# Middle stage of a two-layer Mamba and expert kernel: batch 0's front end by halves, 48 gathers in one row, normalised rows turned back by TensorE

## What is computed

```python
mod = (_silu(L1_c) @ L1_wmod).reshape(L1_c.shape[0], 6, 1, -1)
sa, ca, ga, sb, cb, gb = (mod[:, 0], mod[:, 1], mod[:, 2], mod[:, 3], mod[:, 4], mod[:, 5])
h = _layernorm(x, axis=-1) * (1 + ca) + sa
x = x + ga * _L1_attn_ref(h, ...)
h = _layernorm(x, axis=-1) * (1 + cb) + sb
x = x + gb * _L1_ffn_ref(h, ...)
# _L1_attn_ref: one projection makes z, x|B|C and dt; causal convolution of 4 taps and SiLU on x|B|C;
#   softplus(dt + bias); chunked state recurrence; y * silu(z), RMS norm, output projection;
#   residual is the modulated h itself, then a layer norm with gain and bias
```

## Time and profile before

| | |
|---|---|
| median of 3 runs | 1202.22 us (1201.95 to 1204.38) |
| profiled execution, its own time | 1202.39 us |
| its span, first to last instruction | 1200.5 us |
| busy of the span: PE, DVE, ACT, POOL | 73%, 76%, 52%, 64% |
| mean granted TensorE clock | 0.849 of 2.4 GHz |
| DMA, mean | 100 GB/s |

### The profile page before, as it was taken

One profiled execution on the slowest core, in us unless ns is written; L12 is line 12 of the kernel. 1 busy time (PEld: TensorE's weight loads), 2 busy tenths in 40 slices (PEclk: granted clock), 3 DMA queues, 4 the chain that ended last, 5 costly groups with the idle time before them and its releaser, 6 DMA issues. The chain is left out here.

```text
span 1200.5 us, 14790 instructions
## 1 busy us (share of the span) xinstructions
PE 874.4 (73%) x4148; PEld 554.2 (46%) x4148; DVE 911.2 (76%) x1783; ACT 622.3 (52%) x1381; POOL 771.1 (64%) x518
## 2 busy tenths in 40 slices
PE   7898659886988687751999618787867977339930
PEld 4343324333433332231999603364554666239930
DVE  4896999799979999968677648495986978365512
ACT  4857535665566455525444302748385584246620
POOL 0896698879987999810777378475435445337546
PEclk8998889898999798985899958789987967559975
DMA  6643345434544464442233311211100120142223
GB/s 185 185 146 117 113 156 158 132 126 139 179 133 135 134 183 154 131 146 65 76 93 93 65 51 44 63 35 56 30 25 30 37 66 23 35 176 81 63 62 96
DMA packets 94072, 120.50 MB, mean 100 GB/s; under 512 B 12604, under 2 KB 51972, under 8 KB 93864
## 3 DMA queue, kind: packets, MB, share of 16 engines
q1 hardware_dynamic: 87336, 105.92, 28.6%
q0 software_dynamic: 6656, 13.64, 4.6%
HBM read 105.27 MB, written 14.25 MB: 100 GB/s over the span
## 5 line engine op out<-in xcount | busy, mean ns | idle before, releaser
L678 POOL TENSOR_TENSOR ma_bu<-ma_u,ma_row_b 128x1024 f32<-128x1024 f32 x128 | 299.6, 2363 | 24.8 <-DVE decay_ps L782 16.7
L411 PE MATMUL y_ps<-ma_h,ident 128*128 128x512 f32 x512 | 261.6, 642 | 53.8 <-POOL ma_h L688 34.7
L555 ACT ACTIVATE decay_ps<-ma_delta,negA 128x512 f32<-128x512 f32 x256 | 173.1, 687 | 101.5 <-DVE ma_h L792 98.4
L1208 POOL DMA_INDIRECT s_rows<-xs,take x112 | 124.6, 1112 | 108.2 <-POOLq L952 71.4
L411 PEld LDWEIGHTS y_ps<-ma_h,ident 128*128 128x128 f32 x512 | 98.1, 203 | 195.6 <-issue 98.2
L782 DVE TENSOR_TENSOR_SCAN decay_ps<-decay_ps,ma_bu 128x512 f32<-128x512 f32 x96 | 114.6, 1208 | 24.0 <-ACT decay_ps L555 21.4
L792 DVE TENSOR_TENSOR ma_h<-decay_ps,ma_row_c 128x512 f32<-128x512 f32 x192 | 127.5, 664 | 0.0
L1225 PE MATMUL s_up_ps<-s_xt,s_w 128*128 128x128 f32 x896 | 123.1, 282 | 0.0
L782 DVE TENSOR_TENSOR_SCAN decay_ps<-decay_ps,ma_carry,ma_bu 128x512 f32<-128x512 f32 x96 | 120.5, 1270 | 0.3 <-POOL ma_bu L678 0.3
L1225 PEld LDWEIGHTS s_up_ps<-s_xt,s_w 128*128 128x128 f32 x896 | 113.8, 199 | 0.0
L688 POOL TENSOR_TENSOR ma_h<-ma_h,ma_row_c 128x1024 f32<-128x1024 f32 x32 | 75.2, 2350 | 34.1 <-DVE ma_h L782 32.8
(11 more groups left out here) (317 smaller groups left out, 1798.5 us busy)
## 6 DMA issues: line engine op xcount, KB each, us to landing
ma_row_b<-bc_rows SPq DMA_DIRECT2D x128, 256.0 KB, 3.6
ma_row_c<-bc_rows SPq DMA_DIRECT2D x128, 256.0 KB, 3.3
mi_cs<-cs_rows SPq DMA_DIRECT2D x32, 256.0 KB, 3.3
ys<-s_outs SPq DMA_DIRECT2D x28, 256.0 KB
w<-in_experts SPq DMA_DIRECT2D x1, 4112.0 KB, 13.7
w<-in_experts SPq DMA_DIRECT2D x1, 3072.0 KB, 10.3
xs<-rows SPq DMA_DIRECT2D x4, 512.0 KB, 3.3
out<-X SPq DMA_DIRECT2D x8, 256.0 KB, 2.3
```

Of the source, the lines that this page charges most:

```text
L411: mm = pe.matmul(y_ps[:, j, :], m.ident[:], h[g % HS][:, j, :], start=False, stop=True, skip_group_check=True)
L555: act.activation(decay[s % DS][:], delta[b % 2][:, j, col(c)], ACT.Exp, scale=m.negA0[:, j, n:n + 1]).then_inc(decay_done, 1)
L678: pool.tensor_tensor(bu[g % BUS][:], u[b % 2][:, :, col(c)], both(row_b[g % BS]), ALU.mult).then_inc(bu_done, 1)
L1208: pool.indirect_dma_start(rows[s % ROWS][:], None, m.xs[layer], bass.IndirectOffsetOnAxis(ap=m.take[:, s:s + 1], axis=0)).then_inc(fetched ...
```

## The change

Batch 0's front end is taken out of the rounds and written out ahead of them, by halves of 512 tokens (4 tiles): combine, moments, root, normalise, transposes, raw and x pieces, taps and SiLU of the first half do not wait for the second. The rounds now start at 0. Combine, moments and normalise of batch 1 also stand ahead of the rounds; its transposes and raw pieces stand in steps 0 and 1 of round 0, its x pieces in steps 1 to 4, all its z pieces in step 5, its taps one step later. POOL issues the 48 gathers of batches 0, 1 and 2 first of all.

The rows with scale and shift are no longer made by POOL. PE transposes the modulated `hT` back, by halves (`back10`, `back11`), through the same two banks, and ACT copies them to `rows`. So `modulate`, four broadcast loads and two thirds of `scale_row` and `shift_row` go.

```diff
-LATE = (144, 176)
+LATE = (80, 112)
...
-                for dst, block in ((m.gate[:, 0, 1], 5), (m.gate[:, 1, 1], 11), (m.lng_gate[:], 12), (m.lnb_gate[:], 13),
-                                   (m.shift_row[:, 1], 6), (m.scale_row[:, 1], 7), (m.shift_row[:, 2], 9),
-                                   (m.scale_row[:, 2], 10)):
+                for dst, block in ((m.gate[:, 0, 1], 5), (m.gate[:, 1, 1], 11), (m.lng_gate[:], 12), (m.lnb_gate[:], 13)):
...
-    ROUNDS = range(-3, NBATCH + 2)
+    ROUNDS = range(NBATCH + 2)
+    FIRST_GATHERS = (0, 0, 2, 2, 3, 3, 3, 3)
...
+        if s == 1 and valid(b - 2):
+            out += [("back11", b - 2, 0), ("back11", b - 2, 1)]
         if s == 5 and valid(b + 2):
             out += [("n10", b + 2, 0), ("n10", b + 2, 1)]
+        if s == 6 and valid(b + 2):
+            out += [("back10", b + 2, 0), ("back10", b + 2, 1)]
         if s >= 6 and valid(b + 2):
             out += [("raw", b + 2, 2, s - 6), ("raw", b + 2, 3, s - 6)]
-        if valid(n):
+        if n == 1:
+            if s == 0:
+                out += [("n10", 1, 0), ("n10", 1, 1), ("raw", 1, 2, 0), ("raw", 1, 3, 0)]
+            if s == 1:
+                out += [("raw", 1, 2, 1), ("raw", 1, 3, 1)]
+            if s == 6:
+                out += [("back10", 1, 0), ("back10", 1, 1)]
+            if 1 <= s < 5:
+                out += [("x", 1, (s - 1) // 2, (s - 1) % 2)]
+            if s == 5:
+                out += [("z", 1, j, c) for j in range(HALVES) for c in range(NCOL)]
+        elif valid(n):
...
+    halves = [[("raw", 0, 2, c), ("raw", 0, 3, c), ("x", 0, 0, c), ("x", 0, 1, c)] for c in range(NCOL)]
+    gates = [("z", 0, j, c) for j in range(HALVES) for c in range(NCOL)]
...
             def store_normed(n):
-                sp.wait_ge(modulated11, 2 * n + 2)
+                sp.wait_ge(piece_read, read("back11", n, 1))
...
+            for n in range(3):
+                for i in range(2 * GROUP * GROUPS):
+                    gather(n, i)
...
+                elif kind in ("back10", "back11"):
+                    r = key[2]
+                    pe.wait_ge(piece_read, read("n10" if kind == "back10" else "n11", n, r))
+                    for t in range(r * GROUP, (r + 1) * GROUP):
+                        mm = pe.transpose(bank[:, t % GROUP * P:(t % GROUP + 1) * P], m.hT[:, n, PAD + t * P:PAD + (t + 1) * P],
+                                          m.ident[:])
...
+            piece(("n10", 0, 0))
+            for key in halves[0]:
+                piece(key)
+            piece(("n10", 0, 1))
+            time_steps(0)
+            for key in halves[1][:3]:
+                piece(key)
+            pe.wait_ge(dtv_done, 1)
+            sums(0)
+            for key in halves[1][3:] + gates:
+                piece(key)
+            pe.wait_ge(cum_done, 1)
+            overlap(0)
+            turn(0)
+            for key in rows_back:
+                piece(key)
...
+                elif kind in ("back10", "back11"):
+                    first = n * BT + key[2] * GROUP
+                    ins = act.activation(m.rows[:, first:first + GROUP, :], bank[:].rearrange("p (t d) -> p t d", t=GROUP),
+                                         ACT.Copy)
...
+            root_half(0)
+            read_piece(("n10", 0, 0))
+            for key in halves[0]:
+                read_piece(key)
+            root_half(1)
+            read_piece(("n10", 0, 1))
+            for key in halves[1][:2]:
+                read_piece(key)
+            soften(0)
+            read_piece(halves[1][2])
+            exps(0)
+            for c in range(NCOL):
+                if c == 1:
+                    read_piece(halves[1][3])
+                    for key in gates:
+                        read_piece(key)
+                act.wait_ge(piece_read, read("x", 0, 1, c))
+                act.wait_ge(conv_step, (c + 1) * 2 * TAPS)
+                for j in (2, 3, 0, 1):
+                    xs = xbc[0][j][:, col(c)]
+                    silu = act.activation(xs, xs, ACT.Silu, bias=m.cb1[:, j:j + 1])
+                    if c == 1:
+                        silu.then_inc(silu_done, 1)
+            gate(0)
+            spans(0)
+            decay(0)
+            for key in rows_back:
+                read_piece(key)
+            root(rstd["n10"][:], rstd["n10"][:], n10_var, normed(1), logs, n10_rstd)
...
+            for c in range(NCOL):
+                part = range(c * GROUP, (c + 1) * GROUP)
+                combine(0, c)
+                dve.wait_ge(combined, c + 1)
+                moments(m.X, "n10", n10_var, part)
+                normalize(0, "n10", n10_rstd, c + 1, n10_xn, part)
+            for k in range(TAPS - 1):
+                convolve_half(0, k)
+            bias_steps(0)
+            convolve_half(0, TAPS - 1)
+            make_steps(0)
+            convolve_half(1, 0)
+            cumulated(0)
+            for k in range(1, TAPS):
+                convolve_half(1, k)
+            last_steps(0)
+            combine(1, 0)
+            masked(0)
+            combine(1, 1)
+            inputs(0)
+            dve.wait_ge(combined, 2 * GROUPS)
+            moments(m.X[:, tiles(1), :], "n10", n10_var)
+            normalize(1, "n10", n10_rstd, normed(1), n10_xn)
...
+                    tap = s - 1 if b == 0 else s
+                    if 0 <= tap < TAPS and valid(b + 1):
+                        convolve(b + 1, tap)
+                    if s in ((0, 2) if b == 0 else range(GROUPS)) and valid(b + 2):
+                        combine(b + 2, int(s > 0))
```

More of the change, by code:

```diff
@@ L1397, in pieces @@
         return out
+    halves = [[("raw", 0, 2, c), ("raw", 0, 3, c), ("x", 0, 0, c), ("x", 0, 1, c)] for c in range(NCOL)]
+    gates = [("z", 0, j, c) for j in range(HALVES) for c in range(NCOL)]
     place = {}
+    rows_back = [("back10", 0, r) for r in range(2)]
+    for key in [("n10", 0, 0)] + halves[0] + [("n10", 0, 1)] + halves[1] + gates + rows_back:
+        place[key] = len(place)
     for b in ROUNDS:
@@ L1515, in gather @@
                     ap=m.where[:, k, T:T + 1], axis=0)).then_inc(fetched[G % FETCH], 16)
[L1517 to L1525, removed]
-                                   ).then_inc(done, 1)
             def add_bias(n):
@@ L1554, in _ @@
                     if valid(b + 3):
-                        for i in range(sent, sent + GATHERS[s]):
+                        share = FIRST_GATHERS[s] if b == 0 else GATHERS[s]
+                        for i in range(sent, sent + share):
                             gather(b + 3, i)
-                        sent += GATHERS[s]
-                    if s == 7 and valid(b + 2):
-                        modulate(b + 2, 0, 0, read("n10", b + 2, 1), modulated10)
-                    if s == 0 and valid(b + 1):
-                        modulate(b + 1, 0, 1, read("n10", b + 1, 1), modulated10)
+                        sent += share
                     if s == 3 and valid(b):
                         add_bias(b)
-                    if s in (1, 2) and valid(b - 2):
-                        modulate(b - 2, 1, s - 1, read("n11", b - 2, 1), modulated11)
         @block.tensor
@@ L1799, in _, with root_half @@
                 act.activation(ex, below, ACT.Exp).then_inc(ex_done, 1)
+            def root_half(c):
+                half = rstd["n10"][:, c * GROUP:(c + 1) * GROUP]
+                root(half, half, n10_var, c + 1, logs, n10_rstd)
+            root_half(0)
[27 more added lines that the diff above has]
+            root(rstd["n10"][:], rstd["n10"][:], n10_var, normed(1), logs, n10_rstd)
             for b in ROUNDS:
@@ L1890, in convolve, with convolve_half @@
                     else:
-                        dve.wait_ge(conv_step, n * 2 * TAPS + 2 * (k - 1) + q + 1)
+                        dve.wait_ge(conv_step, convolved(n) + 2 * (k - 1) + q + 1)
                         dve.scalar_tensor_tensor(dst[:], src, tap, dst[:], ALU.mult, ALU.add).then_inc(conv_step, 1)
+            def convolve_half(c, k):
+                for q, j in enumerate(CONV):
+                    src, dst = raw[q][:, c * COL + k:c * COL + k + COL], xbc[0][j][:, col(c)]
+                    tap = m.tap1[:, j, k:k + 1]
+                    if k == 0:
+                        dve.wait_ge(piece_read, read("raw", 0, j, c))
+                        dve.tensor_scalar(dst, src, tap, None, ALU.mult).then_inc(conv_step, 1)
+                    else:
+                        dve.wait_ge(conv_step, c * 2 * TAPS + 2 * (k - 1) + q + 1)
+                        dve.scalar_tensor_tensor(dst, src, tap, dst, ALU.mult, ALU.add).then_inc(conv_step, 1)
             def bias_steps(n):
@@ L1974, in scale_out @@
                 dve.wait_ge(o_done, (G + 1) * GROUP)
-                dve.wait_ge(modulated10, 2 * b + 2)
+                dve.wait_ge(piece_read, read("back10", b, 1))
                 for t in range(GROUP):
```

56 lines of the change are left out of this document (29 added, 27 removed).

## The result

The changed kernel took 1197.83 us (median of 8 runs, 1192.54 to 1199.17) beside 1202.18 for the kernel before: ratio 0.9947, interval 0.9932 to 0.9962. The ratio compares means. By it the kernel is 0.5% or 6 us faster (4.4 us by the medians), where 16 us were forecast, and the time lies just outside the range of 1174 to 1197.

A forecast was written before the change was run, and what follows sets the result against it. Front end read as a chain with no engine full, rounds as fuller. M(0) -23.0, round 0 +7.5, round 1 +0.9, rounds 2 and 3 -3.6, tail +2.8: total -15.4, 1186.9, taken as 1186 us; range 1174 to 1197.

The forecast's parts named there:

- Term 1: Front end: M(0), POOL's line 1544 product for tile 0, comes 23.0 us earlier; ends 15 and 25.
- Convolution and combine only move by a step inside the round: nothing: Round 0: these moves cost nothing, covered by PE's x pieces (3.5 us a step); without that cover 2.5 us.
- Term 3: Rows turned back on PE and ACT: +3.1 us in round 0, +1.9 in round 1, +0.6 each in rounds 2 and 3.
- if PE has fallen to half clock: Upper end for the rows turned back at step 6 of rounds 0 and 1: twice the figure, 10 us.
- The slower rival: Step 6, rounds 0 and 1: two-bank ring delays tile 6's outputs, 9.4 us twice; total 1207; chance 0.07.
- +0.6: Rounds 2 and 3: norm 11's rows turned back at step 1, where ACT has idle time, cost 0.6 us in each.
- Term 4: POOL's sixteen row passes go, no longer stretching DVE: -2.4 us in round 0, -1 in round 1, -4.8 in round 2.
- Term 2: Work moved into round 0: +5 us for batch 1's normalise, transposes and raw pieces, +1.8 for its z pieces in step 5.
- Term 5: Tail: back11 pieces delay scale_out by 1.6 us in round 4 and the logits' read by 1.2 in round 5; ends 1 and 5.
- POOL's last passes vanish, but they ended together with the logits: End of the stage: removing POOL's last passes gains nothing.
- After the stage nothing changes: Everything behind the middle stage: no change in time.
- Less: Rival: PE binds round 0 (7.8 us instead of 5) and step 6 costs its upper end (+5): 1194; chance 0.22.

The follow-up runs named there:

- e14: Changed kernel with the gathers of batches 1 and 2 held on POOL until ACT has read the first half's last x piece: 1197.16 us, ratio 0.9942.
- e15: Kernel before with the turned rows alone, no POOL passes, norm 11 at step 1, norm 10 at steps 2 and 3: 1192.83 us, ratio 0.9901.
- e4: Changed kernel with both combines of batch 2 at steps 0 and 1 of round 0 instead of 0 and 2: 1194.41 us, ratio 0.9911.
- e7: Changed kernel with norm 10 turned at steps 2 and 3 and batch 2's combines at steps 0 and 1, on a 1232 us chip: 5.2 us above e8.
- e8: Kernel of e7 plus batch 1's gate pieces two in step 4, two in step 5, on a 1232 us chip: 5.2 us below e7 by medians.
- e16: Kernel before with the turned rows alone, no POOL passes, norm 11 at step 1, norm 10 at step 6: 1204.12 us, ratio 1.0002.
- e2: Changed kernel with four POOL products that nobody reads added at the end of the stage: 1201.67 us, ratio 0.9988.
- e3: Changed kernel with two POOL products that nobody reads added at the end of the stage: 1198.43 us, ratio 0.9955.
- e11: Same kernel as e8, run again where the kernel before takes 1232 us: 1234.5 us.

## Why the prediction was wrong, step by step

- **Term 1 held.** M(0) came 20.1 us earlier by the start of the stage, 23.0 forecast, ends 15 and 25. Both chains ended together, as worked out. But e14 shows that not all of it is worth its length. By e15 about 6 us of the old front end were the doing of the passes alone.
- **"Convolution and combine only move by a step inside the round: nothing" failed.** This is the largest miss. The cover named was PE's x pieces, while M(4) and M(6) wait for DVE. M(3) to M(4) grew by 5.0 us, M(5) to M(6) by 2.9 (4.0 and 2.7 against the second trace of the kernel before). e4 gets 4.1 of the first back. I had not asked what the combine would stand beside at its new step: the bias pass.
- **Term 3 was mis-sized: 3.1 and 1.9 forecast, 5.4 and 4.0 measured.** The mechanism was right: ACT reads more pieces before it can go on, and PE paces it. The working had PE at full clock; PE came at half clock behind its 7.50 us of idle time. I had named that as the upper end ("if PE has fallen to half clock"), and the sum of 9.4 is close to its 10. The slower rival was another mechanism, outputs of tile 6 behind the third piece that decide M(8). They did come late, but did not decide: its 9.4 us at each of two steps was not paid, and that it equals the measured 9.4 for both together is chance. (Its price also has a slip: the terms that it replaces add up to 9.0, not 8, so 1206.) The "+0.6" for step 1 was too small to be told apart in the table.
- **Term 4 was mis-sized: 8.2 forecast.** e15 shows 0 to 3 us net of the pieces in rounds and tail together (forecast 8.2 less 1.2 for pieces at their small price), and 6.4 in the front end. The stretches went as forecast: in e15 the combine's product takes 4.15 instead of 6.44 us, the normalise 3.1 instead of 4.90, the tap 2.86 instead of 4.95. In the front end and up to M(3) (20.5 us instead of 22.8) that shortened the chain. Round 2, where the other two stand, took 67.5 us beside 68.3 and 67.9: a stretched instruction on DVE is not always a stretched round.
- **Term 2**: the gate pieces held (1.8 forecast; 1.8 from M(6) to M(7), 2.8 by the rounds 0 of e7 and e8). The +5 for batch 1's work was too much. From M(0) to M(3), where it was put, e4 took 21.2 us and e16, which has its combines at the same steps and no passes either, but not this work, 20.5.
- **Term 5 failed in both halves.** M(31) to the logits took 0.2 us more (1.0 in the second trace), not 2.8. "POOL's last passes vanish, but they ended together with the logits", costed at nothing, was worth 5.1 us at the end of the stage. "After the stage nothing changes" was wrong by this gap.

The terms of the profiled execution: M(0) -20.1, round 0 +13.8, round 1 +2.9, rounds 2 and 3 +0.4, tail +0.2, gap -5.1, before and behind the stage -1.9: -9.8, of which the median keeps 4 to 6. The rival "Less" (1194) had the right direction, and step 6 at its upper end was half of its reason. The other half, PE binding round 0, was not what happened. That the total came within 1 us of the range is partly luck: the gap's 5.1 us, which the prediction had at nothing, hide most of what the moved combine and tap cost.

## What to carry to other kernels

Of two chains that end in one instruction, ask what else the engines do while that instruction waits; a milestone that moves 20 us is worth only what the work behind it cannot already use. In a ring of two banks, do not queue more than two pieces between two long blocks of the engine that reads them: it then has to wait while the third and later ones are made, here at half clock. The same pieces cost 5.4 and 4.0 us at step 6 of two rounds and nothing that the traces show at steps 2 and 3. Before you move an instruction by a step "inside its cover", name the engine that the next milestone waits for, and the instructions of other engines that will run beside it.

## What the runs showed of the hardware

- The following stage starts 5.6 us behind POOL's last product but 0.6 behind DVE's last instruction, whichever is later (5.58, 5.56 and 5.58 us in the kernel before, e2 and e3; 0.57 in the changed kernel). By that alone a late pass on POOL that feeds only a store costs up to 5 us.
- A group of four DVE products of 0.98 us took 4.88 beside two POOL instructions with two inputs, of 2.37 and 1.28 us: it lost 3.9 us, about their sum.
- Chips differ by more than the change: the same kernel before takes 1202 to 1205 us on four calls and 1232 on two, with stalls of ACT of up to 21.8 us (e11) in front ends with gathers, and the sign of the change turns with them (0.9947 and 1.0142).
